# Three reorderings in an attention and feed-forward kernel: a GpSimd power behind the low parts, VectorE copies ahead of channel operations, output products that begin with high parts

## The reference

```
h = rmsnorm(layernorm(x), ln_weight)            # per row: (x - mean) * (var + eps) ** -0.5
q, k, v = h @ w_q.T, ctx @ w_k.T, ctx @ w_v.T   # 32 heads of 128, D = 512
p = softmax(q @ k.T + position_bias, masked)    # 128 x 128 per head and batch row
x = x + layernorm(x) + (p @ v) @ w_out.T
x = x + down(silu(gate(y)) * up(y))             # y = layernorm(x); operands rounded to 8 bits per row
x = x + channel_attention(layernorm(x))         # mask = the 76 largest of 128 channels of ctx, then means, maxima, convolution
x = x + lora_mixture(layernorm(x))              # router with 8 experts, the best 2
```

## Time and profile before

| | |
|---|---|
| median of 3 runs | 1042.27 us (1041.65 to 1044.9) |
| time of the profiled execution | 1042.51 us |
| its span | 1040.0 us |
| PE busy | 1001.8 us, 96% |
| PEld busy | 847.7 us, 82% |
| DVE busy | 694.0 us, 67% |
| ACT busy | 513.0 us, 49% |
| POOL busy | 456.4 us, 44% |
| chain that ended last | PE 80%, DVE 8%, issue 5%, POOL 2% |
| granted TensorE clock over the span | 0.997 |

### The profile page before, as it was taken

One profiled execution on the slowest core, in us unless ns is written; L12 is line 12 of the kernel. 1 busy time (PEld: TensorE's weight loads), 2 busy tenths in 40 slices (PEclk: granted clock), 3 DMA queues, 4 the chain that ended last, 5 costly groups with the idle time before them and its releaser, 6 DMA issues.

```text
span 1040.0 us, 18535 instructions
## 1 busy us (share of the span) xinstructions
PE 1001.8 (96%) x6163; PEld 847.7 (82%) x6182; DVE 694.0 (67%) x1835; ACT 513.0 (49%) x1297; POOL 456.4 (44%) x359
## 2 busy tenths in 40 slices
PE   8999999999999999999999999999999999987887
PEld 7888888888888888888888887887888788863464
DVE  7567566656577776768755565657557665769977
ACT  4444544444444555444544354354535635446664
POOL 4555444444444545444434436335342733513431
PEclk9999999999999999999999999999999999999999
DMA  7432233333322223333322313222221322100002
GB/s 265 126 98 85 92 90 97 98 99 99 95 87 86 88 86 98 101 121 128 107 74 87 86 34 103 71 87 60 81 86 35 94 80 87 37 21 22 1 2 81
DMA packets 50413, 87.72 MB, mean 84 GB/s; under 512 B 6368, under 2 KB 15200, under 8 KB 50336
## 3 DMA queue, kind: packets, MB, share of 16 engines
q1 hardware_dynamic: 50336, 86.76, 27.3%
HBM read 84.64 MB, written 2.10 MB: 83 GB/s over the span
## 4 chain that ended last, share of the span: by engine, by line
PE 80%; DVE 8%; issue 5%; POOL 2%; DVEq 2%; ACT 1%; DMA 0%; SPq 0%; POOLq 0%; ACTq 0%
PE pX L1821 15%; PE pX L1823 15%; PE pX L1822 15%; PE pT L2075 6%; PE oacc L1821 5%; PE oacc L1822 5%; PE oacc L1823 5%; PE pS L2007 5%; PE pS L1826 2%; POOL wv_lo L580 1%; PE pT L1996 1%; PE pX L1940 1%; PE pX L1996 1%; DVE silu L1558 1%; PE pX L1826 1%
## 5 line engine op out<-in xcount | busy, mean ns | idle before, releaser
L580 POOL TENSOR_TENSOR wq_lo<-raw_q,wq_hi 128x512 fp32r<-128x512 f32 x64 | 82.6, 1290 | 268.6 <-DVE prob L1439 257.9
L1821 PE MATMUL pX<-wv_lo,cT_hi 128*128 128x256 f32 x512 | 149.4, 292 | 0.2 <-ACT q_sb L761 0.2
L889 ACT ACTIVATE prob<-score,neg_max 128x128 f32<-128x128 f32 x256 | 99.8, 391 | 97.2 <-DVE neg_max L1425 97.2
L1422 DVE TENSOR_TENSOR score<-pS,b_mask 128x512 f32<-128x512 f32 x64 | 44.2, 691 | 153.6 <-PE pS L2007 141.3
L1822 PE MATMUL pX<-wv_hi,cT_lo 128*128 128x256 f32 x512 | 144.1, 281 | 0.0
L1823 PE MATMUL pX<-wv_hi,cT_hi 128*128 128x256 f32 x512 | 144.1, 281 | 0.0
L580 POOL TENSOR_TENSOR wv_lo<-raw_v,wv_hi 128x1024 fp32r<-128x1024 f32 x32 | 77.0, 2407 | 121.5 <-ACT wv_hi L761 121.5
L761 ACT ACTIVATE v_sb<-pX 128x512 f32<-128x512 f32 x64 | 38.2, 597 | 163.3 <-PE pX L1823 163.3
L1821 PE MATMUL pX<-xT_lo,wq_hi 128*128 128x512 f32 x252 | 105.0, 417 | 5.7 <-POOL wq_lo L580 5.0
L1821 PE MATMUL oacc<-wo_lo,aT_hi 128*128 128x512 f32 x256 | 100.5, 393 | 3.3 <-DVE aT_lo L1405 2.2
L1821 PE MATMUL pX<-cT_lo,wk_hi 128*128 128x512 f32 x252 | 102.8, 408 | 0.0
(11 more groups left out here) (342 smaller groups left out, 2371.8 us busy)
## 6 DMA issues: line engine op xcount, KB each, us to landing
raw_k<-in_wk SPq DMA_DIRECT2D x64, 256.0 KB, 2.9
raw_q<-in_wq SPq DMA_DIRECT2D x64, 256.0 KB, 3.6
raw_v<-in_wv SPq DMA_DIRECT2D x32, 512.0 KB, 4.2
raw_o<-in_wo SPq DMA_DIRECT2D x64, 256.0 KB, 2.7
b_raw<-in_bias SPq DMA_DIRECT2D x64, 64.0 KB, 2.8
g_raw<-in_w_gate SPq DMA_DIRECT2D x16, 172.0 KB
g_raw<-in_w_up SPq DMA_DIRECT2D x16, 172.0 KB
f_raw<-in_w_down SPq DMA_DIRECT2D x4, 688.0 KB, 4.3
```

The lines of the kernel that those rows point to most:

```text
L580: g.tensor_tensor(w_lo[c][:], w_raw[c][:], w_hi[c][:].bitcast(F32), ALU.subtract).then_inc(s_w_lo[c], 1)
L889: e = a.activation(prob[:, b, :], score[:, b, :], ACT.Exp, bias=neg_max[:, b:b + 1], accum_out=row_sum[:, b:b + 1])
L1422: v.tensor_tensor(score[:], pS[:].rearrange("p (b s) -> p b s", b=HB), b_mask[:], ALU.add).then_inc(s_scored, 1)
L1821: mm(dst, lh, rl, start=start, stop=False, skip_group_check=lint)
```

## The change

Four places change.

1. The two powers of `early_rsqrt` are parted. That for the third block (`e_zrs`) stays at the front of GpSimd's step. That for the early row (`e_yrs`) comes behind the low parts of queries, outputs and keys and behind `b_mask`, and ahead of `early_split`.
2. On VectorE, in steps with j = 0, the key copy and the copy `pT_sb` come ahead of the two `pick` operations and of both rounds. In the other steps the order stays.
3. `outputs` begins with the four high x high matmuls, one for each batch row, which wait only for `aT_hi`. Then come high x low and low x high for each row, and the wait for `aT_lo` stands ahead of the first low x high.
4. Behind the last step, VectorE's second branch of `e_split` moves behind the sum and the statistics of batch row 4.

```diff
-            def early_rsqrt(n):
+            def early_y_rsqrt(n):
 
                 t = turn(n, -2)
                 if t is not None:
                     pool.wait_ge(s_e_var, t + 1)
                     g.tensor_tensor(e_yrs[:], e_ve[:, 0:1], neg_half[:, 0:1], ALU.pow).then_inc(s_e_rstd, 1)
+
+            def early_z_rsqrt(n):
+
                 t = turn(n, 7)
...
             def step(n, m, odd, half):
-                early_rsqrt(n)
+                early_z_rsqrt(n)
                 pool.wait_ge(s_norm_done, n + 1)
...
                 if odd and unless_last(n + 3):
                     lo("v", m + 2)
+                early_y_rsqrt(n)
...
                 if j == 0:
+                    if unless_last(n + 1):
+                        key_out(n + 1)
+                    dve.wait_ge(s_p_trans, n + 1)
+                    v.tensor_copy(pT_sb[:], pS[:]).then_inc(s_pT, 1)
                     dve.drain()
                     for r in range(2):
...
                 if not end:
                     pick_round(last=j == 3)
-                if unless_last(n + 1):
-                    key_out(n + 1)
-                dve.wait_ge(s_p_trans, n + 1)
-                v.tensor_copy(pT_sb[:], pS[:]).then_inc(s_pT, 1)
+                if j > 0:
+                    if unless_last(n + 1):
+                        key_out(n + 1)
+                    dve.wait_ge(s_p_trans, n + 1)
+                    v.tensor_copy(pT_sb[:], pS[:]).then_inc(s_pT, 1)
...
-            masked(e_split, pX1, 0, HB - 1, s_e_split)
+            early_bank = pX1[:].rearrange("p (k s) -> p k s", k=KT)
+            dve.drain()
+            v.tensor_tensor(e_split[:, 0], early_bank, top[:, 0, :, HB - 1, :], ALU.mult).then_inc(s_e_split, 1)
             residual_of(0)
             token_stats(0, 1)
+            v.tensor_tensor(e_split[:, 1], early_bank, e_split[:, 0], ALU.subtract).then_inc(s_e_split, 1)
...
             def outputs(n, start=False):
-                pe.wait_ge(s_a_lo, n + 1)
+                pe.wait_ge(s_a_hi, n + 1)
                 pe.wait_ge(s_w_lo["o"], n + 1)
                 for b in range(HB):
+                    mm(oacc[b][:], aT_hi[:, b * S:(b + 1) * S], w_hi["o"][:], start=start, stop=False,
+                       skip_group_check=True)
+                for b in range(HB):
                     cols = slice(b * S, (b + 1) * S)
-                    last = three(oacc[b][:], (aT_hi[:, cols], aT_lo[:, cols]), (w_hi["o"][:], w_lo["o"][:]),
-                                 start=start, stop=False, lint=True)
+                    mm(oacc[b][:], aT_hi[:, cols], w_lo["o"][:], start=False, stop=False, skip_group_check=True)
+                    if b == 0:
+                        pe.wait_ge(s_a_lo, n + 1)
+                    last = mm(oacc[b][:], aT_lo[:, cols], w_hi["o"][:], start=False, stop=False,
+                              skip_group_check=True)
```

## The result

| | before | changed |
|---|---|---|
| median | 1042.73 us (6 runs) | 1037.83 us (6 runs, 1034.98 to 1039.92) |
| ratio | | 0.9946, 95% interval 0.9929 to 0.9963 |
| profiled execution, its span | 1042.51, 1040.0 us | 1039.92, 1038.1 us |
| granted TensorE clock, mean | 0.997 | 0.989 |
| PE busy | 1001.8 us | 1005.8 us |

It is faster by 4.9 us where 9.6 were forecast. The time lies 0.8 us outside the range, though on the side that was forecast. The profiled execution is the slowest of the six; the two fastest, 1034.98 and 1035.47, had a mean clock of 0.998, as high as the best of before. PE is busy for 4 us more with the same matmuls: the first sign of where to look.

The account below looks back on a forecast made before the run. TensorE's own work was taken as the bound, with only idle time ahead of matmuls to gain. 8.9 - 1.3 + 1.7 - 0.2 + 0.4 + 0.1 = 9.6 us off 1042.5 gave 1032.9 us; range 1029.5 to 1037.0.

Parts of the forecast that it names:

- 1.6 slow clock: Part 1, step 49: ending the slow stretch behind the 2.10 us stall gains 1.6 us, within part 1's 8.9.
- A slow clock elsewhere: Rival: a longer stand, before the first tail transposes or in step 33, brings one slow stretch; 1034.5 us, chance 0.2.
- rows 5: Earlier profile from 716.98 us: nine matmuls took 3.64 us at low clock against 2.05, a slow stretch priced at 1.6.
- rows 4: Earlier profile: output products waiting for late `aT_lo` behind late scores, 0.53 us too much; part 1 counted three, 1.6 us.
- Step 48, term 1.3: Later `pick` and statistics make TensorE wait 0.3 and about 0.7 us in step 49; with remainders 1.3 us taken back.
- The price of `pick`: Behind the copies on VectorE, both `pick` together were taken to last 1.2 to 2.0 us by step.
- Part 3, term 0.4: Outputs with high parts first: own gain from two remaining waits of 0.2, 0.4 us; its use is cover for part 2.
- Slower by bank changes: Rival: four more `oacc` bank changes in each of 64 output groups cost time; at 0.08 us each 1053 us, chance 0.03.

Follow-up runs that it names:

- e3: Changed kernel plus nine matmuls with unused result in step 63, ahead of the transposes of `prob`: 1034.69 us, 0.9917.
- e7: Changed kernel with the outputs of step 62 alone back in the old order: 1035.80 us, 0.9927.
- e8: Changed kernel plus the nine matmuls in step 63, with `pick` moved to the end of the step before (j = 3): 1031.67 us, 0.9883.
- e9: Changed kernel with `pick` moved to the end of the step before (j = 3), without the nine matmuls: 1031.93 us, 0.9892.
- e12: Changed kernel with the nine matmuls in step 63, run once more on one chip with the unaltered changed kernel: 1035.16 us, 0.9922.
- e6: Kernel before plus the same nine matmuls in step 63: 1043.62 us (12 runs), 1.0011.
- e1: Kernel before with part 1 alone, the power `e_yrs` behind the low parts: 1037.47 us, 0.9942.
- e2: Changed kernel without part 4, so with the tail of before: 1036.51 us, 0.9941.
- e4: Kernel before with part 3 alone, outputs beginning with high parts: 1040.85 us (8 runs), 0.9981.
- e11: Changed kernel run once more, unaltered: 1036.75 us (1034.98 to 1039.16), 0.9937.
- e5: Kernel before with part 2 alone, the copies ahead of `pick`: 1052.33 us, 1.0088.
- e10: Kernel before with `pick` moved to the end of the steps with j = 3 and nothing else: 1038.93 us, 0.9955.

## Why the prediction was wrong

**The step that failed** is the handling of the slow clock. Part 1 counted its end as a sure gain ("1.6 slow clock") and the sum held none in its place; the rival "A slow clock elsewhere" had it once, at the price of rows 5, with a chance of 0.2, "before the first tail transposes" or in step 33. Measured: it fell at neither of these. Step 33 stood for 2.01 us, as forecast, and the clock stayed up; the tail transposes stood for 1.61 in the changed profile, and for the forecast 2.1 in the five where the clock had stayed up at step 63 (e3, e7, e8, e9, e12), with no fall right behind. It fell one wait earlier, at the last `prob`, where part 3 had joined 0.78 and 1.69 to 2.46 us. And the price was not 1.6: `prob` to `t_y` took 2.19 us more than in e3. By the profile of the changed kernel against that of before: 8.4 gained in the attention, 1.3 lost ahead of it, 2.05 at step 63, 2.25 in the tail, together 2.8 sooner at VectorE's last operation, where the executions differ by 2.6 and their spans by 1.9.

The 1.6 us itself was misread. It took all that the earlier trace rows lacked against full pace for the clock. e6, at full clock in the same place, stands for 0.55 us at `aT_lo` there, the fourth follower of the kind of rows 4, which the slow clock had covered. So 1.1 us was the clock and 0.5 the wait. The sum stays the same, for part 1 removes both, but only the 0.5 is a gain in every execution.

How much is the clock in all? Fifteen of the 51 executions of before that ran beside e1 to e12 had a mean clock of 0.998, with a median span of 1040.3 us; the two changed ones there had 1032.1 and 1033.7. So at equal clock the change is worth about 7.4 us, an estimate from two executions, of the 8.5 that the forecast has without the clock's 1.1; the 0.7 of step 48 below is most of the rest. The remaining loss is that the changed kernel runs at a lower mean clock.

Shown is that the low clock at step 63 goes with the joined stand: with it four of five profiles (changed, e2, e4, e11, not e9) have it, without it none of nine; e3 and e12 fill the stand and are 2.4 us faster in the median; e6 puts the matmuls where the stand was short and gains nothing. e7, which parts the stand, points the same way, though its time is not clear of the changed kernel's. Not shown is what decides in the single execution. The same holds in step 49: two kernels with the order of before there, e4 and e6, stood for 2.11 and 2.12 us, and the clock fell in the first and not in the second:

```profile
716.00:717.00 1.00, 1.00 (x4) 0.81 (x3) 0.91 (x3) 0.00 (x0) 1.00 (x2) 0.50 0.60 225
```

```profile
717.00:718.00 1.00, 1.00 (x6) 0.80 (x5) 0.88 (x2) 0.00 (x0) 1.00 (x1) 1.00 0.73 231
```

So the clock's share of the earlier trace rows was a gain in some executions only. The Trainium skill, TensorE: Matmul & The Clock Gate, section "What's actually happening", says the windows run free of the kernel; stands of equal length with both outcomes agree. What stays open: the tail's 2.25 us. All fourteen profiles have a low clock from 986 to 1007 us on, at a stand of 1.96 to 1.98 us that no kernel here touches. In six it lasts 3.4 us (before, e2, e3, e5, e10, e12) and begins 1.4 to 2.2 us after the stand's end; in eight it lasts 6.8 us (e1, with nothing changed at the end, and e8, with the matmuls, among them) and begins at most 0.8 us after it (in e8 and e9 even before). The tail from `t_y` is 96.1 to 96.6 us long in the six and 97.9 or more in the eight. So the tail's loss goes with when the clock falls; no experiment moved that on purpose. Nor do the medians of e8 and e9, 0.3 us apart, settle whether the matmuls help there: the means are 1.1 us apart, two of e9's five executions had mean clocks of 0.991 and 0.993 where e8's four had 0.995 to 0.997, and so few can't tell the two apart.

**Part 1** held: -1.03, -2.01, -2.01 at steps 37, 43 and 55 against 1.06, 2.05 and 2.07, with the waits gone as said. The power was hidden: VectorE's first use of the row, at 718.86 us in step 49, had no wait.

**Step 48, term 1.3**, was 2.0, as 1.88 us came instead of 2.6 (with 0.2 of part 3 in it). The working names only 0.3 + 0.7 for it; nothing is given for the other 0.3. The scores of step 49 came about as reckoned: 716.3 less the 1.48 us gained up to there is 714.8, and they started at 715.03. But behind them `e_gate`, from 717.19, took 1.75 us where it took 1.02 before, with GpSimd's second `e_split`, which part 1 had also made earlier, beside it from 716.91 to 718.20; ScalarE's `e_hq` and six transposes came after it: 1.77 us of wait for 0.7. I had named the follower and not followed it through. That `e_split` is what slowed `e_gate` was not tested alone.

**Part 2** held: step 60 gave 1.69 for 1.7; steps 32 and 33 lost 0.17 for 0.2, as reckoned: `aT_lo` late, and some 1.1 us of it covered (part 3 alone gains 1.12 there). The price of `pick`, 1.2 to 2.0 us, missed on both sides: in steps 24, 32, 48 and 60 it took 2.16 to 2.23 us, beyond it, and in nine others 1.02 to 1.06 (step 8 above; 2.6 before in steps 8 to 20, but 0.49 in 36, 44 and 56). It got longer in two ways. In 36 and 48 part 1 alone does it, by GpSimd's earlier row (e1, `pick` in its old place: 2.60 and 2.59); in 44 and 56 the move alone does it (e5: 1.03 and 1.02, where e1 has 0.49). The Trainium skill, SBUF — State Buffer, section "SBUF: two separate sides", has this as a lock for the whole instruction; the rows agree (0.49 with GpSimd idle in e9, 2.16 in step 48 of the changed kernel, ending 0.15 us after `wo_lo`).

**Part 3, term 0.4**, is wrong in both directions: -2.4 us of attention by itself, 1.12 of them in steps 32 and 33 and the rest mostly where part 1 gains as well, and the joined stand. "Its own gain is small" looked at the four waits only in sum and left out the 1.27 us of the earlier trace rows. **Part 4**: 0.14 for 0.1 up to `t_y`, and nothing by the end (e3). **Slower by bank changes**: excluded, loads in `oacc` stay 0.23 us apart and steps 2 to 31 don't move.

## What to carry over

A wait that is removed ahead of another wait is not gained, it is joined to it; list the stands of TensorE that become longer, and reckon with its clock at half speed behind each of about 2 us or more, as long as those that had it here, for several microseconds and in some executions only. A few superfluous matmuls in such a stand were the cheaper choice here; leaving the earlier wait may be. Where a busy GpSimd slows an operation, look for a place in which it stands rather than move the operation up or down beside it: the same two instructions took 0.49 us there in all of e10's steps, and at least 1.02 behind the copies.

## What the runs showed of the hardware

- Equal stands have unequal consequences: 2.45 us at step 63 with a clock of 0.50 behind it (e4) and 1.00 (e9); 3.16 us in e5 was followed by 0.50, 2.34 by no fall, 2.56 by 0.50. In the tail a stand of 1.96 to 1.98 us had a fall at it in all fourteen profiles.
- A low stretch in step 49 cost 1.1 us where a wait behind it was covered (before against e6), one of twice the length cost 2.19 at step 63 (changed against e3).
- VectorE's MAX and MATCH_REPLACE took 0.49 and 0.28 us beside a busy GpSimd as beside an idle one, while `pick`, with two operands in SBUF, went from 0.49 to 2.16 and more.
- A change with the same work per step moved the mean clock of the span from 0.997 to 0.989, and PE's busy time by 4 us: busy time alone would have said that TensorE had more to do.
